# A three-pass half-precision split of the expert layer's first products, with rows turned by the DMA, in a fused attention and mixture-of-experts kernel

## Chip, cores and metric

The kernel runs on 1 core of a Trainium2 chip. The metric is the device time in microseconds (us) of one execution.

## The reference, cut to what matters

Input x has 8 batches of 512 tokens of 128 features (4096 tokens). First attention with 16 heads of 64, causal, with one null key and value, and a layer norm of the sum:

```
x1 = layernorm(x + attention(x))
```

Then a mixture of 32 experts (4 chosen per token out of 4 of 8 groups, at most 640 rows per expert) beside one shared expert, and a second layer norm:

```
w, idx = gate(x1)                     # softmax, grouped top 4, weights normalized
xe = x1 rows by expert                # (32, 640, 128)
h = silu(xe @ w1) * (xe @ w3)         # the first products, 128 to 128
out = (h @ w2) * weight of the row    # added back to the token's row: y
z = silu(x1 @ sw1) * (x1 @ sw3) @ sw2
result = layernorm(x1 + y + z)
```

All is float32.

## The kernel before

All engines follow one list of steps, written by `plan`: each engine runs through `steps` and takes the ones that are its own, in order, so a wait holds up all that stands behind it on that engine. The orders of the attention stage (`ORDER` to `ORDER4`) are written out by hand; the smaller work of a finished batch (`finish`) is put into the slots `place` and `slow`.

- Attention, batch by batch. TensorE, in float16 halves, is busy nearly throughout. ScalarE takes exponentials and copies, VectorE row maxima and low halves, GpSimd the low halves of the probabilities (L2289), SyncE moves keys and queries between partitions (L2458, L2425) and turns the halves of x with one transposing DMA per batch (L2403).
- `finish(b)`: layer norm to X1 (float32), x1 turned on TensorE (L1393), copied to X1T and stored in HBM as columns (L2477, `x1_t`), gate, top 4, places. `payload` on ScalarE (L1690) writes each x1 row four times into PAY (128 float32 values, then the place number and the weight, `ROW` = 130 words), and GpSimd scatters them by 16 indirect DMAs a batch into `xe_rows` (L2322).
- Between the stages SyncE reloads x1's columns (L2483), the weights of the first experts (L2370, then L2491 and L2494) and the rows of the first two experts (L2379). The last batch is finished in two halves of 8 scatters. Five `shared up` / `shared down` steps and the first two experts are worked in between.
- The expert loop, x_ from 2 to 29, in this order on TensorE: `turn(x_+1)` turns the next expert's 640 rows by five float32 transposes into PSUM (L1137), VectorE (`turned`, L1751 and L1752) copies them to XET; `dense_down` (L1488) of the step before; `hidden(x_)` (L1154), four float32 products of 128x320; `dense_up` (L1479), two float32 products of 128x512; `product(x_-1)` (L1167). The dense steps, one in each of x_ = 6 to 24, are the shared expert and two experts computed for all tokens. ScalarE: silu (L1543, L1708) and weighted copies to OUT (L1551). VectorE: products with silu (L1758, L2145) and the dense sums (L2163). GpSimd: five indirect DMAs an expert that scatter OUT's rows to `y_rows` (L2332). SyncE: weights of x_+3 and rows of x_+4; the rows wait until the scatters of expert x_-2 have landed. OUT has 4 buffers and the rows have 6.
- After the last scatter and the last dense sum the token's four rows are loaded, summed (L1523, L1531, L1532) and normalized.

Of the kernel before, what the change touches and what calls it, by code (L numbers as in the profile page):

```python
# [16 lines left out]
N = NB * T  # L17
# [132 lines left out]
def plan(count):  # L150
# [6 lines left out]
        "c_pz", "c_as", "c_dz", "c_nm", "c_sh", "c_na", "c_ps", "c_dl", "c_sc0", "c_lq", "c_k20", "c_k21", "c_k22", "c_ll", "c_xd")}  # L157
# [245 lines left out]
    def finish(b, *half):  # L403
# [59 lines left out]
        if whole or half == (1,):  # L463
            mark("xts", b, by="c_xts", n=16)
# [10 lines left out]
        for h in half:  # L475
            step("payload", b, h)
            mark("payx", b, h, by="c_aj")
            mark("payi", b, h, by="c_pg")
        yield from wait(5)
        for name in ("group max", "group top", "group drop", "masked", "top", "top index"):  # L480
            dv(name)
            yield
        dv("gate sum")
# [42 lines left out]
        if whole:  # L526
            for h in (0, 1):
                step("payload", b, h)
                mark("payx", b, h, by="c_aj")
                mark("payi", b, h, by="c_pg")  # L530
                yield
            ready.append(b)
# [246 lines left out]
    for x_ in range(NA):  # L779
        step("load early rows", x_)  # L780
    gate_free = (st_free[0], st_free[1])
# [43 lines left out]
    step("early turn", 0)  # L825
# [3 lines left out]
    step("early turn", 1)  # L829
# [11 lines left out]
    step("first turn")  # L841
# [11 lines left out]
def program(nc, ctx, x, Wq, Wk, Wv, Wo, null_k, null_v, logit_scale, wg, w1, w2, w3, sw1, sw2, sw3, out):  # L853
# [8 lines left out]
    x1t_d = nc.dram_tensor("x1_t", (C, N), F32, kind="Internal").ap()  # L862
# [105 lines left out]
    def at(*key):  # L968
# [19 lines left out]
    s_turn, s_xet, s_hid, s_sil, s_hs, s_o, s_oc = (  # L988
        sem(n) for n in ("s_turn", "s_xet", "s_hid", "s_sil", "s_hs", "s_o", "s_oc"))
# [52 lines left out]
    ph1, X1TA, HZ, ph2 = flat(K1), flat(K2), flat(Q1), flat(Q2)  # L1042
# [7 lines left out]
    XE = ph2[:, 0:3900].rearrange("p (s k r) -> p s k r", s=6, k=5)  # L1050
    XET = PF[:, 0:2, 0:640]
    SIL = Y[:, :, :, :].rearrange("p s a b -> p s (a b)")
    xe_e = xe.rearrange("(e p k) r -> e p k r", e=E, k=5)
# [28 lines left out]
    BUF = [t[:, h:h + 2048] for t in (X1TA, ph2, HZ, ph1) for h in (0, 2048)]  # L1082
# [39 lines left out]
    def tensor(e):  # L1122
# [1442 lines left out]
```

## Time and profile before

| | us |
|---|---|
| three runs | 977.4, 980.4, 985.9 |
| median | 980.4 |
| span of the profiled execution (first to last instruction) | 977.5 |
| attention, one batch of the middle | 75.7 |
| end of attention to first scatter of expert outputs | 640 to 695 |
| expert stage, scatters of experts 0 to 29 | 695 to 937 |
| load, sum, norm and store | 941 to 977 |

TensorE is busy for 859.0 us of the span, GpSimd 673.5, VectorE 654.3, ScalarE 616.8; the mean granted TensorE clock is 0.943 of full speed. Only the span stands for the profiled execution; what lies outside it is at most the few us by which the runs differ from it.

### The profile page before, as it was taken

What the parts mean: (1) busy time and instruction counts of PE and PEld (TensorE: products, weight loads), DVE (VectorE), ACT (ScalarE), POOL (GpSimd) and SP (SyncE); (2) the same over time, 40 slices, a digit from 0 to 9 for tenths busy, and PEclk for the clock granted to TensorE, in tenths of its full rate; (3) what the DMA queues carried; (4) which work ended last, traced back from release to release, by engine and by line L of the source; (5) the groups of instructions that cost most, each with busy time, mean ns of one, the idle gap of its engine ahead of it and who ended that gap; (6) DMA issues with size and microseconds to landing.
All of it is one profiled execution on the core that took longest, in us unless ns stands there. A gap on an engine that the chain in (4) does not pass through costs nothing. (4 is left out here: it accounts for less than half of the span.)

```text
span 977.5 us, 25690 instructions
## 1 busy us (share of the span) xinstructions
PE 859.0 (88%) x9439; PEld 633.9 (65%) x9439; DVE 654.3 (67%) x2448; ACT 616.8 (63%) x1189; POOL 673.5 (69%) x580
## 2 busy tenths in 40 slices
PE   5789999999999999999999999766688888888654
PEld 2367777777777777777777777654465666666422
DVE  7757788987987987987987986836243434343217
ACT  3668889888888888888898787733132323233305
POOL 7656665699698699699689689346665555556636
PEclk9989999999999999999999999978798989899968
DMA  5787788645444454354354342016333323333147
GB/s 160 182 255 234 231 243 220 177 107 134 97 119 111 101 135 108 89 151 107 73 141 122 72 117 64 21 51 197 119 96 100 96 79 95 95 101 99 39 191 252
DMA packets 104428, 126.62 MB, mean 130 GB/s; under 512 B 22077, under 2 KB 65426, under 8 KB 103408
## 3 DMA queue, kind: packets, MB, share of 16 engines
q1 hardware_dynamic: 95408, 109.25, 40.8%
q0 software_dynamic: 8896, 15.74, 5.2%
q8 instruction: 75, 1.23, 0.5%
q14 instruction: 49, 0.40, 0.1%
HBM read 33.68 MB, written 41.58 MB: 77 GB/s over the span
## 5 line engine op out<-in xcount | busy, mean ns | idle before, releaser
L2289 POOL TENSOR_TENSOR PL<-PF,PH 128x1280 f16<-128x1280 f32 x121 | 317.8, 2626 | 107.2 <-ACT PH L1632 63.7
L1854 DVE CUSTOM_DVE_ANT_0 JUNK<-PS,M 128x256 f16<-128x256 f32 (+3 forms) x512 | 225.2, 485 | 39.5 <-PE PS L1265 35.8
L1626 ACT ACTIVATE PF<-PS 128x512 f32<-128x512 f32 (+1 forms) x384 | 192.8, 520 | 80.3 <-PE PS L1298 75.4
L2332 POOL DMA_INDIRECT y_rows<-BIG,Q x150 | 145.7, 972 | 99.3 <-ACT BIG L1551 57.4
L1632 ACT ACTIVATE PH<-PF 128x1280 f16<-128x1280 f32 x128 | 162.2, 1267 | 0.6
L2322 POOL DMA_INDIRECT xe_rows<-PAY,DEST x128 | 129.3, 1010 | 42.9 <-issue 27.7
L1291 PE MATMUL PS<-Q,K 128*128 128x512 f16 (+3 forms) x512 | 148.6, 300 | 9.2 <-DMA Q<-MROW 4.9
L1315 PE MATMUL PS<-VH,PH 128*128 128x65 f16 x1280 | 141.3, 195 | 13.0 <-DVE Y L1896 8.5
L1317 PE MATMUL PS<-VH,PL 128*128 128x65 f16 x1280 | 141.3, 194 | 1.2 <-issue 1.2
L1315 PEld LDWEIGHTS PS<-VH,PH 128*128 128x128 f16 x1280 | 119.6, 98 | 35.0 <-issue 24.5
L1316 PE MATMUL PS<-VL,PH 128*128 128x64 f16 x1280 | 141.3, 194 | 0.0
L1316 PEld LDWEIGHTS PS<-VL,PH 128*128 128x128 f16 x1280 | 118.8, 99 | 2.7
L1317 PEld LDWEIGHTS PS<-VH,PL 128*128 128x128 f16 x1280 | 119.2, 98 | 0.4 <-issue 0.4
L1296 PE MATMUL PS<-Q,K 65*128 65x128 f16 (+2 forms) x384 | 106.0, 276 | 0.0
L1298 PE MATMUL PS<-Q,K 128*128 128x128 f16 x512 | 102.6, 220 | 0.0
L1294 PE MATMUL PS<-LATER,IDB 128*128 128x64 bf16 x512 | 98.7, 193 | 0.0
L1543 ACT ACTIVATE Y<-PS 128x640 f32<-128x640 f32 x30 | 21.1, 704 | 106.6 <-remote 56.8
L1154 PE MATMUL PS<-PF,K 128*128 128x320 f32 x240 | 80.1, 481 | 9.2 <-DVE Q L2122 4.9
L1154 PEld LDWEIGHTS PS<-PF,K 128*128 128x128 f32 x240 | 49.2, 217 | 29.4 <-issue 16.2
L1291 PEld LDWEIGHTS PS<-Q,K 128*128 128x128 f16 x512 | 50.7, 99 | 24.2 <-ACT PF L1626 8.7
L1265 PE MATMUL PS<-K,Q 64*128 64x256 f16 (+3 forms) x512 | 63.1, 305 | 0.1
L1551 ACT ACTIVATE BIG<-PS,Q 128x128 f32<-128x128 f32 x150 | 42.3, 374 | 30.8 <-PE PS L1167 16.9
(252 smaller groups left out, 2027.5 us busy)
## 6 DMA issues: line engine op xcount, KB each, us to landing
K<-KH SPq DMA_DIRECT2D x128, 128.0 KB, 2.3
Q<-QH SPq DMA_DIRECT2D x128, 128.0 KB, 2.4
xe_rows<-PAY SPq DMA_DIRECT2D x20, 520.0 KB, 4.2
Q<-xe_rows SPq DMA_DIRECT2D x30, 325.0 KB
K<-KL SPq DMA_DIRECT2D x64, 128.0 KB, 2.3
Q<-QL SPq DMA_DIRECT2D x64, 128.0 KB, 2.3
y_rows<-PAY SPq DMA_DIRECT2D x16, 512.0 KB, 4.9
K<-in_L_ffn_w_dram SPq DMA_DIRECT2D x96, 64.0 KB
```

The costliest lines, as they stand in the source:

```text
L1154: i = e.matmul(PS[:, bank + hf, 0:320], EW[:, x_ % 4, m, :], XET[:, x_ % 2, hf * 320:(hf + 1) * 320], start=True, stop=True)
L1291: e.matmul(PS[:, k, o:o + LEN[i]], K1[:, u % 4, ab, pp, block], Q1[:, u % 4, ab, pp, i * 128:512], start=True, stop=False)
L1296: e.matmul(PS[:, k, o + 128:o + LEN[i]], K2[0:65, u % 4, ab, pp, block], Q2[0:65, u % 4, ab, pp, i * 128 + 128:512], start=False, stop=False)
L1315: e.matmul(PS[:, 4, o:o + 65], PH[:, n % PBUF, p], VH[:, vs, i, h, :], start=(i == 0), stop=False)
L1316: e.matmul(PS[:, 4, o:o + 64], PH[:, n % PBUF, p], VL[:, vs, i, h, :], start=False, stop=False)
L1317: r = e.matmul(PS[:, 4, o:o + 65], PL[:, n % PBUF, p], VH[:, vs, i, h, :], start=False, stop=(i == q))
L1626: e.activation(PF[:, n % PBUF, c0:c0 + width], PS[:, k, 0:width], ACT.Exp).then_inc(s["c_exp"], 1)
L1632: e.activation(PH[:, n % PBUF, :], PF[:, n % PBUF, :], ACT.Copy).then_inc(s["c_hc"], 1)
L1854: e.tensor_tensor_reduce(JUNK[:, n_ttr % 2, 0:width], PS[:, base + ab, c0:c0 + width], M0[:, 512 - width:512], 1.0, -3e38, ALU.add, ALU.ma ...
L2289: e.tensor_tensor(PL[:, n % PBUF, :], PF[:, n % PBUF, :], PH[:, n % PBUF, :], ALU.subtract).then_inc(s["c_lp"], 1)
L2322: e.indirect_dma_start(out=xe[:, :] if b < NB - 1 else xe[0:(NE - NA) * CAP, :], out_offset=bass.IndirectOffsetOnAxis(ap=DEST[:, q, k:k + ...
L2332: e.indirect_dma_start(out=y4[:, :], out_offset=bass.IndirectOffsetOnAxis(ap=XE[:, x_ % 6, k, 128:129].bitcast(I32), axis=0), in_=OUT[:, x ...
```

## The change

x1 is no longer kept for the expert stage as float32: `x1 high` (ScalarE) writes its float16 rounding and `x1 low` (VectorE) the float16 rounding of the rest, side by side in the first of the four payload rows. SyncE copies that row to the other three by DMA (`payload`, six DMAs a batch of 128 partitions x 1 KB, waited for by the scatters), and stores x1's rows to HBM (`x1_rows`, 512 bytes a token). In the expert stage the rows arrive turned: `dma_start_transpose` loads an expert's 640 rows x 256 halves into XT, and a second small DMA the place numbers and weights (XI); x1's columns for the shared and dense steps come by transposing DMAs too (512 x 256 each). The float32 transposes on TensorE and their copies by VectorE go. The weights w1, w3 of each expert are split into high and low float16 (`high_weights` on ScalarE, `low_weights` on VectorE, 128x256 each, one expert ahead; the shared and dense ones once). Each first product becomes three float16 products (high x high, high x low of x1, low x high), summed in PSUM. The second products stay float32. Orders of steps are otherwise kept.

```diff
@@ -429,6 +429,11 @@
+        def rows(h):
+            step("payload", b, h)
+            mark("payx", b, h, by=("c_px0", "c_px1")[h], n=48)
@@ -524,11 +534,18 @@
+            step("x1 high", b)
+            mark("x1h", b, by="c_aj")
+            yield
+            dv("x1 low")
+            yield
...
-                step("payload", b, h)
-                mark("payx", b, h, by="c_aj")
+                rows(h)
+                step("place numbers", b, h)
...
+            step("x1 store", b)
+            mark("xts", b, by="c_xts", n=16)
@@ -1047,10 +1067,22 @@
-    XE = ph2[:, 0:3900].rearrange("p (s k r) -> p s k r", s=6, k=5)
+    XT = ph2[:, 0:3840].bitcast(F16).rearrange("p (s w n) -> p s w n", s=6, w=2)
+    XI = ph2[:, 3840:3900].rearrange("p (s k r) -> p s k r", s=6, k=5)
...
-    xe_e = xe.rearrange("(e p k) r -> e p k r", e=E, k=5)
+    xe_t = xe.bitcast(F16).rearrange("(e n) r -> e n r", e=E)
+    XHI = PAY[:, :, 0, 0:64].bitcast(F16)
+    XLO = PAY[:, :, 0, 64:128].bitcast(F16)
+    def split_of(t):
+        return t.bitcast(F16).rearrange("p (w n) -> p w n", w=2)
+    EWS = [split_of(PF[:, j, 0:256]) for j in (0, 1)]
@@ -1126,21 +1158,23 @@
-        def turn(x_):
-            w.wait_ge(l_xe[x_ % 6], 16 * (x_ // 6 + 1))
-            w.wait_ge(s_xet, x_)
-            w.wait_ge(*at("zt", 1))
-            if x_ >= NA:
-                w.wait_ge(*at("z", 3))
-            bank_free(misc_end)
-            for k in range(5):
-                i = e.transpose(five(0, k), XE[:, x_ % 6, k, 0:128], IDF[:, :])
-            i.then_inc(s_turn, 1)
+        def three(out, halves, m, x_of, free):
+            high, low = halves[:, 0, 128 * m:128 * m + 128], halves[:, 1, 128 * m:128 * m + 128]
+            for o, n in free:
+                e.matmul(out(o, n), high, x_of(0, o, n), start=True, stop=False)
+                e.matmul(out(o, n), high, x_of(1, o, n), start=False, stop=False)
+            for o, n in free:
+                i = e.matmul(out(o, n), low, x_of(0, o, n), start=False, stop=True)
+            return i
...
-            w.wait_ge(l_w[x_ % 4], 48 * (x_ // 4 + 1))
-            w.wait_ge(s_xet, x_ + 1)
+            w.wait_ge(l_xe[x_ % 6], 32 * (x_ // 6 + 1))
+            w.wait_ge(s_wsh, x_ + 1)
+            w.wait_ge(s_wsl, x_ + 1)
...
+            if x_ == 0:
+                w.wait_ge(*at("zt", 1))
@@ -1150,15 +1184,15 @@
-                for hf in range(2):
-                    i = e.matmul(PS[:, bank + hf, 0:320], EW[:, x_ % 4, m, :], XET[:, x_ % 2, hf * 320:(hf + 1) * 320],
-                                 start=True, stop=True)
-                i.then_inc(s_hid, 1)
+                three(lambda o, n: PS[:, bank + o // 320, 0:n], EWS[x_ % 2], m, lambda k, o, n: XT[:, x_ % 6, k, o:o + n],
+                      ((0, 320), (320, 320))).then_inc(s_hid, 1)
...
+                bank_free(misc_end)
+                w.wait_ge(l_w[x_ % 4], 48 * (x_ // 4 + 1))
@@ -1440,14 +1473,13 @@
-                e.matmul(PS[:, one, :], SW[:, 0, :], X1TA[:, t], start=True, stop=True)
-                e.matmul(PS[:, two, :], SW[:, 1, :], X1TA[:, t], start=True, stop=True).then_inc(s["c_ph"], 1)
+                for m, bank in ((0, one), (1, two)):
+                    i = three(lambda o, n: PS[:, bank, 0:n], SWS, m, lambda k, o, n: X1TA[:, b, k, :], ((0, 512),))
+                i.then_inc(s["c_ph"], 1)
...
-                if b >= 2:
-                    w.wait_ge(s_xet, 2)
@@ -1544,12 +1571,17 @@
-            w.wait_ge(l_xe[y_ % 6], 16 * (y_ // 6 + 1))
+            w.wait_ge(l_xe[y_ % 6], 32 * (y_ // 6 + 1))
...
-                             scale=XE[:, y_ % 6, k, 129:130]).then_inc(s_oc, 1)
+                             scale=XI[:, y_ % 6, k, 1:2]).then_inc(s_oc, 1)
+        def high_weights(x_):
+            w.wait_ge(l_w[x_ % 4], 48 * (x_ // 4 + 1))
+            w.wait_ge(s_hid, 2 * (x_ - 1))
+            e.activation(EWS[x_ % 2][:, 0, :], EW[:, x_ % 4, 0:2, :].rearrange("p m n -> p (m n)"), ACT.Copy).then_inc(s_wsh, 1)
@@ -1680,16 +1711,21 @@
-            elif name == "payload":
-                b, half = a
-                w.wait_ge(*at("scat", b - 1, half))
+            elif name == "x1 high":
+                b, *half = a
+                q0, q1 = span(*half)
+                for h in half or (0, 1):
+                    w.wait_ge(*at("scat", b - 1, h))
...
-                for key in parts_of("normalize", b, half):
-                    w.wait_ge(*at(*key))
-                for q in (2 * half, 2 * half + 1):
-                    i = e.activation(PAY[:, q, :, 0:128], X1[:, 4 * b + q, :].unsqueeze(1).broadcast_to((128, 4, 128)),
-                                     ACT.Copy)
-                i.then_inc(s["c_aj"], 1)
+                w.wait_ge(*at("xts", b - 1))
+                w.wait_ge(*at("normalize", b, *half))
+                e.activation(XHI[:, q0:q1, :], X1[:, 4 * b + q0:4 * b + q1, :], ACT.Copy).then_inc(s["c_aj"], 1)
+            elif name == "shared split":
+                w.wait_ge(l_sw, 48)
+                w.wait_ge(*at("ng", LAST))
+                e.activation(SWS[:, 0, :], SW[:, 0:2, :].rearrange("p m n -> p (m n)"), ACT.Copy).then_inc(s_dwh, 1)
+            elif name == "early split":
+                high_weights(*a)
@@ -1745,11 +1790,11 @@
-        def turned(x_):
-            w.wait_ge(s_turn, x_ + 1)
+        def low_weights(x_):
+            w.wait_ge(s_wsh, x_ + 1)
...
-            e.tensor_copy(XET[:, x_ % 2, 0:384], PS[:, 0, 0:384])
-            e.tensor_copy(XET[:, x_ % 2, 384:640], PS[:, 1, 0:256]).then_inc(s_xet, 1)
+            e.tensor_tensor(EWS[x_ % 2][:, 1, :], EW[:, x_ % 4, 0:2, :].rearrange("p m n -> p (m n)"), EWS[x_ % 2][:, 0, :],
+                            ALU.subtract).then_inc(s_wsl, 1)
@@ -2109,12 +2153,21 @@
-            elif name == "early turn":
-                turned(*a)
+            elif name == "x1 low":
+                b, *half = a
+                q0, q1 = span(*half)
+                w.wait_ge(*at("x1h", b, *half))
+                e.tensor_tensor(XLO[:, q0:q1, :], X1[:, 4 * b + q0:4 * b + q1, :], XHI[:, q0:q1, :],
+                                ALU.subtract).then_inc(s["c_dv"], 1)
...
@@ -2164,18 +2216,22 @@
+        def low_dense(d):
+            src = DW[:, d, 0:2, :] if d < ND else AW[:, d - ND, 0:2, :]
+            w.wait_ge(s_dwh, d + 2)
+            e.tensor_tensor(DWS[d][:, 1, :], src.rearrange("p m n -> p (m n)"), DWS[d][:, 0, :],
+                            ALU.subtract).then_inc(s_dwl, 1)
...
-            if x_ == NA:
-                times(x_)
-            if x_ < NE - 1:
-                turned(x_ + 1)
+            if x_ + 1 < NE:
+                low_weights(x_ + 1)
...
-            if x_ > NA:
-                times(x_)
+            times(x_)
...
+                low_dense(WEIGHTS[k])
@@ -2374,9 +2430,10 @@
-            w.wait_ge(s_turn, x_ - 5)
+            w.wait_ge(s_hid, 2 * (x_ - 5))
...
-            e.dma_start(XE[:, x_ % 6, :, :], xe_e[expert(x_)]).then_inc(l_xe[x_ % 6], 16)
+            e.dma_start_transpose(XT[:, x_ % 6, :, :], xe_t[expert(x_)][:, 0:256]).then_inc(l_xe[x_ % 6], 16)
+            e.dma_start(XI[:, x_ % 6, :, :], xe_i[expert(x_)][:, :, 128:130]).then_inc(l_xe[x_ % 6], 16)
@@ -2470,17 +2527,27 @@
-            elif name == "x1 copy" and a != [NB - 1, 0]:
-                b = a[0]
-                for key in parts_of("x1t", b):
+            elif name == "payload":
+                b, half = a
+                q = slice(*span(half))
+                key = (b,) if b < NB - 1 else (b, half)
+                w.wait_ge(*at("x1h", *key))
+                w.wait_ge(*at("x1 low", *key))
+                w.wait_ge(*at("scat", b - 1, half))
+                for k in range(1, 4):
+                    i = e.dma_start(PAY[:, q, k, 0:128], PAY[:, q, 0, 0:128])
+                    i.then_inc(s[("c_px0", "c_px1")[half]], 16)
+            elif name == "x1 store":
+                b, = a
+                for key in parts_of("x1 low", b) + parts_of("x1h", b):
...
-                e.dma_start(x1t_d[:, b * 512:(b + 1) * 512], X1T[:, :]).then_inc(s["c_xts"], 16)
+                e.dma_start(x1_b[b], PAY[:, :, 0, 0:128].bitcast(F16)).then_inc(s["c_xts"], 16)
...
-                e.dma_start(X1TA[:, b * 512:(b + 1) * 512], x1t_d[:, b * 512:(b + 1) * 512]).then_inc(l_xa[b], 16)
+                e.dma_start_transpose(X1TA[:, b, :, :], x1_d[b * 512:(b + 1) * 512, :]).then_inc(l_xa[b], 16)
```

`dense_up` calls `three` in the same way; the splits of the shared and dense weights and the place numbers' step on GpSimd are left out here.

## Rows read from the trace of the kernel before

**Rows 1.** Busy time by stage: stretch, its length, busy us of each engine, TensorE's clock, DMA share, GB/s
```profile
225.70:301.40 75.70, 74.59 (x1043) 56.85 (x1042) 64.43 (x264) 64.05 (x117) 62.25 (x49) 1.00 0.44 111
...
745.00:897.00 152.00, 132.74 (x625) 96.39 (x625) 61.51 (x137) 46.57 (x124) 86.17 (x90) 0.90 0.32 93
...
941.00:977.50 36.50, 23.99 (x54) 11.21 (x54) 18.97 (x92) 13.16 (x32) 18.67 (x18) 0.78 0.78 288
```

**Rows 2.** Timeline of GpSimd, expert stage: start, us, instruction, idle before it
```profile
712.13 0.97 POOL L2332 DMA_INDIRECT y_rows<-BIG,Q  x1 [2.80 <-ACT BIG L1551]
...
743.08 0.97 POOL L2332 DMA_INDIRECT y_rows<-BIG,Q  x1 [3.46 <-ACT BIG L1551]
...
760.12 0.97 POOL L2332 DMA_INDIRECT y_rows<-BIG,Q  x1 [0.68 <-issue]
...
769.40 0.97 POOL L2332 DMA_INDIRECT y_rows<-BIG,Q  x1 [3.20 <-ACT BIG L1551]
...
896.66 0.97 POOL L2332 DMA_INDIRECT y_rows<-BIG,Q  x1 [2.91 <-ACT BIG L1551]
...
935.82 0.97 POOL L2332 DMA_INDIRECT y_rows<-BIG,Q  x1 [0.30 <-issue]
```

**Rows 3.** Timeline, TensorE in one pass of the expert loop, full clock
```profile
752.89 0.71 PE L1137 MATMUL PS<-IDF,Q 128*128 128x128 f32 x5
...
753.66 1.16 PE L1488 MATMUL PS<-SW,Q 128*128 128x128 f32 x8
...
754.65 2.32 PE L1154 MATMUL PS<-PF,K 128*128 128x320 f32 x8
...
756.81 1.88 PE L1479 MATMUL PS<-K 128*128 128x512 f32 x4
...
758.53 1.28 PE L1167 MATMUL PS<-K 128*128 128x128 f32 x10
```

**Rows 4.** The same timeline one pass later, VectorE and ScalarE behind TensorE
```profile
763.37 0.56 DVE L1751 COPY PF<-PS 128x384 f32<-128x384 f32 x1 [3.95 <-remote]
...
767.68 0.70 ACT L1543 ACTIVATE Y<-PS 128x640 f32<-128x640 f32 x1 [6.80 <-remote]
```

**Rows 5.** Timeline, TensorE in the pass after that, half clock
```profile
771.07 1.91 PE L1488 MATMUL PS<-K,Q 128*128 128x128 f32 x8
```

**Rows 6.** Timeline of TensorE, attention: two neighbouring float16 products
```profile
232.84 0.39 PE L1234 MATMUL PS<-XHL,WKH 128*128 128x512 f16 x1
...
233.06 0.38 PE L1234 MATMUL PS<-XHL,WKL 128*128 128x512 f16 x1
```

**Rows 7.** SyncE's timeline at a transposing DMA (256 KB)
```profile
270.41 1.27 SPq L2403 DMA_TRANSPOSE XHL<-BIG  x1
```

**Rows 8.** Busy time in the us in which its packets run, columns as in rows 1
```profile
272.00:273.00 1.00, 1.00 (x32) 0.93 (x29) 1.00 (x4) 0.88 (x3) 1.00 (x1) 1.00 1.02 201
```

**Rows 9.** Timeline of SyncE between the stages
```profile
656.68 3.20 SPq L2483 DMA_DIRECT2D K<-x_t  x7
659.92 6.12 SPq L2370 DMA_DIRECT2D K<-in_L_ffn_w_dram  x12
...
671.86 0.85 SPq L2379 DMA_DIRECT2D Q<-xe_rows  x2
...
693.10 3.18 SPq L2379 DMA_DIRECT2D Q<-xe_rows  x2
```

**Rows 10.** Timeline of GpSimd: the last of the 16 scatters of the last batch
```profile
690.79 0.97 POOL L2322 DMA_INDIRECT xe_rows<-PAY,DEST  x1 [0.30 <-issue]
```

**Rows 11.** The page, DMA issues: KB each, median us from issue to landing
```profile
K<-KH SPq DMA_DIRECT2D x128, 128.0 KB, 2.3
```

**Rows 12.** The payload copies' line: ns min/median/max, first and last start
```profile
L1690 ACT ACTIVATE PAY<-X x32: 610/614/661, 186.1 to 669.3; 128x512 f32<-128x512 f32 x32
```

**Rows 13.** The waits in the attention stage: us in total, times, longest
```profile
PE PS L1291 <- DMA Q<-MROW: 2.3, 3, 1.0
```

**Rows 14.** The chain that ended last: start, us, what
```profile
939.90 1.14 DVE X L2163 x4
...
941.18 9.74 PE PS L1523 x16
```

More of the change, by code:

```diff
@@ L474, in finish @@
         mark("ex", b, *half, by="c_aj")
-        for h in half:
-            step("payload", b, h)
-            mark("payx", b, h, by="c_aj")
-            mark("payi", b, h, by="c_pg")
+        if not whole:
+            step("x1 high", b, *half)
+            mark("x1h", b, *half, by="c_aj")
+            step("place numbers", b, *half)
+            mark("payi", b, *half, by="c_pg")
         yield from wait(5)
@@ L482, in finish @@
             yield
+        if not whole:
+            dv("x1 low")
+            rows(half[0])
+            if half == (1,):
+                step("x1 store", b)
+                mark("xts", b, by="c_xts", n=16)
         dv("gate sum")
@@ L780, in plan @@
         step("load early rows", x_)
+    step("shared split")
     gate_free = (st_free[0], st_free[1])
@@ L824, in plan @@
         next(parts[b])
-    step("early turn", 0)
+    step("early split", 0)
+    step("early split", 1)
     next(parts[2])
@@ L828, in plan @@
     step("early hidden", 0)
-    step("early turn", 1)
+    step("early split", 2)
     next(parts[3])
@@ L840, in plan @@
     next(parts[4])
-    step("first turn")
     next(parts[4])
@@ L1424, in tensor @@
                 i.then_inc(s["c_pm"], 1)
-            elif name == "first turn":
-                turn(NA)
             elif name == "shared up":
                 b, = a
-                t = slice(b * 512, (b + 1) * 512)
                 w.wait_ge(l_xa[b], 16)
                 w.wait_ge(l_sw, 48)
+                w.wait_ge(s_dwh, 1)
+                w.wait_ge(s_dwl, 1)
                 if b < 2:
@@ L1458, in tensor @@
                 i.then_inc(s["c_pz"], 1)
-            elif name == "early turn":
-                turn(*a)
             elif name == "early hidden":
@@ L1478, in dense_up @@
             for m, bank in ((0, one), (1, two)):
-                e.matmul(PS[:, bank, :], weights(d, m), X1TA[:, t], start=True, stop=True).then_inc(s_dup, 1)
+                three(lambda o, n: PS[:, bank, 0:n], SWS if d == SHARED else DWS[d], m, lambda k, o, n: X1TA[:, b, k, :],
+                      ((0, 512),)).then_inc(s_dup, 1)
         def dense_down(i, rows):
             d, b = DENSE[i]
+            w.wait_ge(l_dw, 48 * (ND + NA))
             w.wait_ge(s_dh, i + 1)
@@ L1714, in scalar @@
                 copies(x_)
+            for k in WEIGHTS_AT.get(x_, ()):
+                high_dense(WEIGHTS[k])
             if x_ in DENSE_AT:
@@ L1763, in shared_add @@
             w.wait_ge(*at("down", b))
-            w.wait_ge(*at("payx", b, 1))
-            for key in parts_of("xT1", b):
+            for key in parts_of("x1h", b) + parts_of("x1 low", b) + parts_of("xT1", b):
                 w.wait_ge(*at(*key))
@@ L2151, in dense_add @@
                 w.wait_ge(*at("z", b))
-            w.wait_ge(*at("payx", b, 1))
-            for key in parts_of("xT1", b):
+            for key in parts_of("x1h", b) + parts_of("x1 low", b) + parts_of("xT1", b):
                 w.wait_ge(*at(*key))
@@ L2306, in gpsimd @@
                 e.tensor_tensor(RS[:, q], VE[:, q], MHALF[:, q], ALU.pow).then_inc(s["c_pg"], 1)
-            elif name == "payload":
+            elif name == "place numbers":
                 b, half = a
@@ L2498, in sync @@
             if x_ > NA:
[L2499 removed]
+                w.wait_ge(l_xe[x_ - 1], 32)
             load_rows(x_)
```

63 lines of the change are left out of this document (35 added, 28 removed).

## The prediction

> **What bounds the kernel now.** I read the busy times by stage first, then GpSimd's timeline in the expert stage, then one pass of the loop on TensorE. In attention TensorE is busy for 74.6 of 75.7 us a batch [rows 1]: that stage is TensorE's, and nothing on ScalarE, VectorE or SyncE shortens it. In the expert stage the scatters are the clock to read. They follow each other at 0.97 + 0.30 = 1.275 us while OUT is full, so five cost 6.38 us; the first scatter of expert 2 is at 712.1, of expert 6 at 743.1, of expert 24 at 896.7, the last one at 935.8 [rows 2]. That is 7.74 us an expert from 2 to 6, 8.53 from 6 to 24, and 39.2 us from there to the last scatter, 29 steps on. The gaps end with ScalarE's copies [rows 2], and these wait for TensorE: it, not GpSimd, bounds the dense stretch (132.7 of 152 us busy) [rows 1]. A pass at full clock has 6.75 us of it: turn 0.55 + 0.33 to the next group, dense_down 0.89, hidden 2.15, dense_up 1.72, product 1.11 (from start to start of the groups; a group's own time has a tail that overlaps the next) [rows 3].
>
> But three passes take 3 x 8.53 = 25.6 us, not 20.3. In one of three VectorE and ScalarE get TensorE's results late: the copy of the turned rows waits 3.95 us and silu 6.80 us for something the trace doesn't name, though TensorE's records lie where they should [rows 4]; the pass after it runs at half clock (dense_down's group 1.91 instead of 1.16 us) [rows 3, 5]. The scatters show a pass of 9.3 us (760.12 to 769.40) [rows 2]; with one of 6.75 the third has 9.6, so about 2.5 us and 2.8 us are lost in each three passes. It begins when GpSimd goes on from one expert's scatters to the next without a pause (0.68 us at 760.12) [rows 2]. I don't know its cause; it is what the prediction depends on.
>
> **The change, part by part.**
> TensorE, expert loop. The turn goes (0.88 us with its gap) [rows 3]. Hidden: 4 float32 products become 12 float16 ones. Two neighbouring float16 products of 512 columns start 0.216 us apart [rows 6], so one of 320 columns is worth 0.135 and hidden 1.63 us instead of 2.15; dense_up 6 x 0.216 = 1.29 instead of 1.72. dense_down of the step before now stands right behind product and waits for three copies by ScalarE, which the turn covered: I take the same 0.88 us of waiting. A pass: 0.88 + 0.89 + 1.63 + 1.29 + 1.11 = 5.8 us, under the scatters' 6.38. With neither late results nor half clock the pace would be GpSimd's 6.38.
>
> VectorE and ScalarE, loop. VectorE loses 0.97 us of copies and gets a subtraction of 128x256; ScalarE gets a copy of 128x256. Bounds of each: 0.37 (0.56 scaled down by width) and 0.61 [rows 4, 12]. Both engines are busy for 62 and 47 of 152 us [rows 1], so I cost them at nothing; they are done one expert ahead, behind no wait that isn't a pass old. The wait for hidden's first group goes from VectorE's copy to a DMA: one round trip fewer between TensorE and VectorE (three a pass become two), so a late pass loses less.
>
> Pace. I take 5.8 us for a pass that isn't disturbed, and still one late and one half-clock pass, each with two thirds of the old loss and a loss that GpSimd's backlog of 0.6 us a pass doesn't hide: about 7.2 us an expert. Lower bound 6.38, upper bound the present 8.53. From 6 to 24: 18 x 7.2 = 129.6 instead of 153.6: **-24.0 us** (-38.8 to 0).
>
> SyncE between the stages, a loss. Its queue is in order. Seven loads of x1's columns take 3.20 us of issue; turned they are transposing DMAs of 1024 packets like x's, 1.27 us each: 8.9 [rows 7, 9]. The weights stay: 659.9 to 671.9 [rows 9]. The first two rows loads take 0.85; turned they are 1.25 times x's, 1.6, with 0.4 for the numbers: 4.0. So SyncE is free at 656.7 + 8.9 + 12.0 + 4.0 = 681.6 instead of 672.7. Behind it stands the new `payload` of the last batch's first half: three moves, 0.5 us each, landing 2.3 us after the last issue [rows 11]: 685. GpSimd's scatters wait for it; the 16th starts 15 x 1.275 later, at 704.1 instead of 690.8 [rows 10], 13.3 us late. The rows of expert 2 are asked for 2.3 us after the last scatter's start now (693.1) [rows 9, 10], then at 706.4, and are there by 711. But GpSimd has experts 0 and 1 to scatter from 705.4 to 718.2, ready since, so expert 2's first scatter is at about 718.4 instead of 712.1: **+6.3 us** (0 if SyncE issues faster, +13 if nothing closes up). From 2 to 6, no dense steps, GpSimd has backlog and runs at 6.38: 25.5 instead of 31.0: **-5.5 us** (-5.5 to 0).
>
> End. The last dense sum ends at 941.0, 4.2 us after the last scatter [rows 2, 14]. TensorE's tail is now shorter and starts earlier, so the scatters' landing (936.8 + 1.4) would be last: **-2.5 us** (-2.8 to 0). The final stage's 36.5 us [rows 1] stay.
>
> Attention. ScalarE gives up 4 copies of 0.61 us a batch [rows 12] for one; VectorE gets one of 512 columns; neither sets the pace [rows 1]. SyncE gets 6 moves a batch at some 0.6 us, behind waits for `x1 high` and `x1 low`; key and query moves and the row of maxima stand behind them. TensorE has waited for that row 3 times, 2.3 us in all [rows 13]. I take **+1 us** (0 to +35, seven batches at 5). Indirect scatters now wait for a DMA, but GpSimd has 13 us of slack a batch [rows 1].
>
> Transposing DMAs as such. x's 256 KB are issued in 1.27 us, and in the us from 1.6 us after the issue on the queues move at 201 GB/s [rows 7, 8]: some 3.4 us in all, 4.3 for an expert's 320 KB. They are asked for some four passes ahead, so they are hidden; the source there was SBUF, though, and no row has one from HBM.
> The Trainium skill (VectorE: DVE Perf Modes, The three transpose paths) gives 1309 ns for a 128x128 transpose by DMA; x's move has eight such tiles and the trace has it far faster than eight times that, while the same skill (Advanced Engine Details and Errata, X-Bar Transpose) calls these DMAs as fast as regular ones. By the first an expert's ten tiles would be an estimated 13 us and the kernel over 100 us slower; by the second nothing changes in the sum.
>
> Sum: -24.0 + 6.3 - 5.5 - 2.5 + 1.0 = -24.7 on the span of 977.5: 952.8. The median of the runs is 2.9 us above that span: **955.7 us**.
>
> **Rivals.**
> *A, the pace doesn't move.* The late results and the half clock set 8.5 us, not TensorE's work. For it: a lighter pass leaves GpSimd even less pause, the state in which the lateness begins [rows 2, 4]. Against: a third of the round trips go. Then +6.3 - 5.5 + 1: 982 us.
> *B, GpSimd's pace throughout*, no late passes: a further -14.8: 941 us.
> *C, row loads become the bound (the slower side).* Five DMAs an expert instead of four on SyncE, one transposing from HBM, one of 8-byte pieces. If a load takes over twice the 4.3 us of the SBUF case, the pace is over 8.5, the point from which it decides; at 10 us it is 27 x (10 - 7.2) = +76: 1030 us. For it: no row shows such a source. Against: rows 7 and 8. The skill's 1309 ns a tile is this case.
> *D, attention slips* because SyncE's in-order queue delays the row of maxima [rows 13]: 5 us in each of seven batches: 990 us.
> *E, TensorE stays at half clock* since it is busy for less: hidden 3.3, dense_up 2.6, dense_down 1.6, product 2.2, waits 0.9: 10.6 us a pass (its slow groups are those of [rows 5]): +61 on 955.7: 1017 us.
>
> **Chances.** Forecast 0.60, B 0.13, A 0.12, C 0.07, D 0.05, E 0.03. Faster by over 1% (below 970.6; about 1% is what a measurement tells from no change): forecast and B, 0.73; within 1%: A, and a forecast that falls short, 0.13; slower 0.14. The range takes B's time and A's with their doubts: 937 to 985; the forecast alone 943 to 970.
>
> **What would show it.** Scatters of expert 2 at 716 to 721 and of expert 24 at 868 to 875; SyncE's first row load near 678, the last batch's first scatter near 685; pairs of expert scatters without a pause more often than now; VectorE without waits of 4 us for a turn; attention at 75.7 us a batch. The prediction is wrong if the scatters stay 8.5 us apart with TensorE idle (A), if hidden waits for DMA landings (C), if a batch takes over 77 us (D), or if the granted clock between 745 and 890 is under 0.7 (E).

## The result, and the profile after

The changed kernel takes 1026.8 us (median of four runs, 1025.5 to 1030.0), the kernel before 979.8 beside it: a ratio of 1.0475, 95% interval 1.0437 to 1.0513. It is slower by 47 us (46.2 between the two profiled spans) where I forecast 24.7 us less.

The profiled execution spans 1023.7 us instead of 977.5. Four landmarks cut it up, the same that the prediction used. In both kernels SyncE's first load of x1 between the stages waits for the end of attention; before it was at 656.68 [rows 9].

SyncE's timeline of the changed kernel:

```profile
692.90 1.30 SPq L2550 DMA_TRANSPOSE K<-x_rows  x1
...
717.62 0.58 SPq L2436 DMA_DIRECT2D Q<-xe_rows  x1
718.64 4.00 SPq L2538 DMA_DIRECT2D PAY<-PAY  x6
```

GpSimd's timeline of the changed kernel, the lines that answer to [rows 10] and [rows 2]: the last scatter of x1 rows, then the first scatters of experts 2, 6 and 24, and the last one:

```profile
744.39 0.97 POOL L2378 DMA_INDIRECT xe_rows<-PAY,DEST  x1 [0.30 <-issue]
...
758.43 0.97 POOL L2388 DMA_INDIRECT y_rows<-BIG,Q  x1 [0.30 <-ACT BIG L1578]
...
795.09 0.97 POOL L2388 DMA_INDIRECT y_rows<-BIG,Q  x1 [4.14 <-ACT BIG L1578]
...
945.79 0.97 POOL L2388 DMA_INDIRECT y_rows<-BIG,Q  x1 [1.46 <-ACT BIG L1578]
...
986.71 0.97 POOL L2388 DMA_INDIRECT y_rows<-BIG,Q  x1 [0.30 <-issue]
```

| stretch | before | after | difference | forecast |
|---|---|---|---|---|
| start to first x1 load (attention) | 656.7 | 692.9 | +36.2 | +1.0 |
| from there to expert 2's first scatter | 55.4 | 65.5 | +10.1 | +6.3 |
| experts 2 to 6 | 31.0 | 36.7 | +5.7 | -5.5 |
| experts 6 to 24 | 153.6 | 150.7 | -2.9 | -24.0 |
| from there to the end | 80.8 | 77.9 | -2.9 | -2.5 |
| sum | 977.5 | 1023.7 | +46.2 | -24.7 |

So there are two questions: who takes 36 us in attention, and what happened to the 24 us of the expert loop.

**Attention.** The page of the changed kernel, its costliest groups (busy, mean ns, idle just before and what ended it):

```profile
L2378 POOL DMA_INDIRECT xe_rows<-PAY,DEST x128 | 129.0, 1008 | 103.9 <-DMA PAY<-PAY 61.5
...
L1299 PE MATMUL PS<-K,Q 64*128 64x256 f16 (+3 forms) x512 | 63.8, 308 | 21.7 <-DVE MXV L1898 18.0
```

and the same two groups on the page of the kernel before:

```profile
L2322 POOL DMA_INDIRECT xe_rows<-PAY,DEST x128 | 129.3, 1010 | 42.9 <-issue 27.7
...
L1265 PE MATMUL PS<-K,Q 64*128 64x256 f16 (+3 forms) x512 | 63.1, 305 | 0.1
```

GpSimd sits idle for 61.5 us ahead of scatters of x1's rows until the new copies of the payload row have landed, and TensorE waits 18.0 us for VectorE's row maxima (MXV); before, there was no such wait. The timeline of one batch, lines of four engines put in order of time, shows both:

```profile
351.22 2.61 POOL L2345 TENSOR_TENSOR PL<-PF,PH 128x1280 f16<-128x1280 f32 x1 [0.91 <-issue]
352.11 2.27 DVE L2160 TENSOR_TENSOR PAY<-X,PAY 128x512 f16<-128x512 f32 x1 [0.46 <-ACT PAY L1722]
355.05 0.39 PE L1299 MATMUL PS<-K,Q 64*128 64x256 f16 x4 [2.32 <-DVE MXV L1898]
355.75 1.99 SPq L2538 DMA_DIRECT2D PAY<-PAY  x3
360.49 1.03 POOL L2378 DMA_INDIRECT xe_rows<-PAY,DEST  x1 [6.66 <-issue]
365.56 0.19 PE L1349 MATMUL PS<-VH,PH 128*128 128x65 f16 x1 [1.81 <-issue]
```

VectorE's subtraction for x1's low half (L2160) takes 2.27 us. It began while GpSimd worked on the low halves of p (L2345) and ended 0.55 us after GpSimd had ended at 353.83. So it is in each of the first six batches (2.27 us each, always beside such an operation of GpSimd). In the seventh GpSimd stands idle at that time, and the same subtraction is short:

```profile
669.55 0.68 DVE L2160 TENSOR_TENSOR PAY<-X,PAY 128x512 f16<-128x512 f32 x1
```

The Trainium skill (SBUF — State Buffer, SBUF: two separate sides) has a rule for this that I had not used: a VectorE operation with two SBUF inputs and a GpSimd operation that reads SBUF lock each other out for a whole instruction. By that rule the subtraction has to stand behind GpSimd's; the trace agrees (2.27 us beside 0.68). Then the DMA copies are issued at 355.75, GpSimd has stood still since 353.83, and the scatter goes at 360.49. The first scatter of a batch waits like this for 6.3 to 7.5 us in six batches, and for 17.8 and 16.0 in the last two. Behind it in GpSimd's queue stand the next low halves of p (362.81 to 365.46), for which the products of L1349 wait until 365.56.

**Expert loop.** The windows of the changed kernel, columns as in [rows 1], at the same clock times and at the end:

```profile
745.00:897.00 152.00, 102.39 (x574) 74.22 (x574) 47.42 (x104) 50.17 (x136) 89.53 (x91) 0.81 0.49 102
990.00:1023.70 33.70, 22.62 (x52) 9.46 (x51) 18.82 (x91) 13.16 (x32) 18.67 (x18) 0.91 0.84 309
```

The first window is not the same work as before: here experts 0 to 6 fill its first 50 us. Experts 6 to 24, which had 132.7 busy us of TensorE [rows 1], now run from 795 to 945, with 107.9 at a granted clock of 0.88 (the row stands with e4 below). So TensorE's work did fall, and still an expert takes 8.37 us. The late results of [rows 4] are there: TensorE's products of hidden end at 812.76, and ScalarE's silu starts 5.8 us later, held by something that the trace does not name (it writes `remote`). TensorE's line, then ScalarE's:

```profile
812.33 0.43 PE L1168 MATMUL PS<-Q,PF 128*128 128x320 f16 x2
...
818.58 0.70 ACT L1570 ACTIVATE Y<-PS 128x640 f32<-128x640 f32 x1 [6.46 <-remote]
```

TensorE waits for ScalarE's copies ahead of dense_down, and goes in and out of half clock (1.96 us for a group that takes 1.13 at full clock):

```profile
872.90 1.96 PE L1520 MATMUL PS<-K,Q 128*128 128x128 f32 x8 [3.15 <-ACT BIG L1578]
...
881.05 1.13 PE L1520 MATMUL PS<-K,Q 128*128 128x128 f32 x8 [1.32 <-ACT BIG L1578]
...
889.24 1.30 PE L1520 MATMUL PS<-K,Q 128*128 128x128 f32 x8 [3.03 <-ACT BIG L1578]
```

### The profile page after: what moved, and what is told of

Read it like the earlier page. It is cut to its first block, busy times and chain, and to the rows that moved or that the text cites. A ratio compares the mean times of both kernels' runs of the same rounds, so it can differ in the third digit from the quotient of the medians.

```text
span 1023.7 us, 25899 instructions
## 1 busy us (share of the span) xinstructions
PE 832.3 (81%) x9461; PEld 611.4 (60%) x9461; DVE 653.1 (64%) x2432; ACT 618.3 (60%) x1201; POOL 675.4 (66%) x580
## 4 chain that ended last, share of the span: by engine, by line
PE 52%; ACT 9%; issue 9%; SPq 8%; another core or an unknown queue 7%; DMA 6%; DVE 5%; POOL 3%; ACTq 0%; POOLq 0%; DVEq 0%
PE PS L1268 6%; PE PS L1325 5%; PE PS L1299 4%; PE PS L1349 3%; PE PS L1378 3%; PE PS L1332 3%; PE PS L1330 3%; PE PS L1351 3%; PE PS L1350 3%; PE PS L1282 2%; SPq L2515 2%; PE PS L1379 2%; PE PS L1201 2%; PE PS L1520 2%
## 5 line engine op out<-in xcount | busy, mean ns | idle before, releaser
L2345 POOL TENSOR_TENSOR PL<-PF,PH 128x1280 f16<-128x1280 f32 x121 | 318.0, 2628 | 103.3 <-ACT PH L1664 67.0
L2388 POOL DMA_INDIRECT y_rows<-BIG,Q x150 | 148.4, 989 | 93.9 <-ACT BIG L1578 54.2
L2378 POOL DMA_INDIRECT xe_rows<-PAY,DEST x128 | 129.0, 1008 | 103.9 <-DMA PAY<-PAY 61.5
L1349 PE MATMUL PS<-VH,PH 128*128 128x65 f16 x1280 | 141.8, 196 | 19.8 <-issue 8.5
L1349 PEld LDWEIGHTS PS<-VH,PH 128*128 128x128 f16 x1280 | 119.9, 98 | 44.9 <-issue 25.5
L1803 DVE TENSOR_TENSOR K<-PS,Y 128x640 f32<-128x640 f32 x30 | 24.7, 824 | 73.9 <-PE PS L1168 27.0
L1201 PE MATMUL PS<-K 128*128 128x128 f32 x300 | 45.7, 307 | 27.9 <-issue 9.3
L1325 PEld LDWEIGHTS PS<-Q,K 128*128 128x128 f16 x512 | 50.5, 99 | 25.7 <-ACT PF L1658 10.3
```

The costliest lines, as they stand in the source:

```text
L1325: e.matmul(PS[:, k, o:o + LEN[i]], K1[:, u % 4, ab, pp, block], Q1[:, u % 4, ab, pp, i * 128:512], start=True, stop=False)
L1349: e.matmul(PS[:, 4, o:o + 65], PH[:, n % PBUF, p], VH[:, vs, i, h, :], start=(i == 0), stop=False)
L2345: e.tensor_tensor(PL[:, n % PBUF, :], PF[:, n % PBUF, :], PH[:, n % PBUF, :], ALU.subtract).then_inc(s["c_lp"], 1)
L2378: e.indirect_dma_start(out=xe[:, :] if b < NB - 1 else xe[0:(NE - NA) * CAP, :], out_offset=bass.IndirectOffsetOnAxis(ap=DEST[:, q, k:k + ...
L2388: e.indirect_dma_start(out=y4[:, :], out_offset=bass.IndirectOffsetOnAxis(ap=XI[:, x_ % 6, k, 0:1].bitcast(I32), axis=0), in_=OUT[:, x_ % ...
```

## The experiments

Eighteen runs, in five groups of three or four, each group on one chip beside the kernel before. For attention the theories are S (GpSimd waits for the payload DMAs), V (VectorE's subtraction stands behind GpSimd) and Q (SyncE's queue delays the other moves); for the expert loop L (late results set the pace), C (the clock does) and rival C of the prediction (row loads). A batch is the time from the first scatter of x1 rows of one batch to that of the next, as a mean over five; it was 75.8 us before and 81.8 after. Several kernels leave out part of the work, as their expectations say; they are timed only to learn what that part costs.

### Attention

**e1**: the payload rows written by ScalarE.

```diff
-                for k in range(1, 4):
-                    i = e.dma_start(PAY[:, q, k, 0:128], PAY[:, q, 0, 0:128])
+                for q in (2 * half, 2 * half + 1):
+                    i = e.activation(PAY[:, q, 1:4, 0:128].bitcast(F16), ...broadcast_to((128, 3, 256)), ACT.Copy)
```

> The changed kernel with one part undone: rows 1 to 3 of the payload are written by ScalarE again (four float16 copies of 128x768 a batch) instead of six DMAs on SyncE. A batch of attention takes 81.9 us in the changed kernel and 75.7 in the one before. Theory S (GpSimd's in-order queue waits for the payload DMAs and the low halves of p behind it come late): a batch falls to about 77 to 78, the kernel to about 990. Theory V (VectorE's subtraction of 128x512 takes 2.27 us because it stands behind GpSimd's, and TensorE waits 2.3 us for the row maxima behind it): most of the 6.2 us stays, a batch 80 or more, the kernel about 1010 to 1020. Theory Q (SyncE's queue is what delays keys, queries and the row of maxima): a batch at 75.7, the kernel about 980.

Measured: a batch 79.4 us; 990.8 us beside 970.5, ratio 1.022 (1.013 to 1.032). That is between what theories S and V foretold. Of theory S it is not all: GpSimd still waits 3 us a batch, now for ScalarE's copies.

```profile
271.57 1.03 POOL L2386 DMA_INDIRECT xe_rows<-PAY,DEST  x1 [3.03 <-ACT PAY L1728]
```

**e2**: DMAs as they are, the scatters later in the list.

```diff
             mark("xts", b, by="c_xts", n=16)
+            for _ in range(4):
+                yield
             ready.append(b)
```

> The changed kernel with the scatters of a batch put into GpSimd's list four slots of the batch's smaller work later, all DMAs kept. Theory S: GpSimd no longer waits for the payload DMAs, a batch at 77 to 79 us instead of 81.9, the kernel about 1000. Theory Q: the DMAs are still on SyncE's queue, so a batch stays at 80 to 82 us and the kernel at 1020 or more.

Measured: a batch 78.3 us, 1010.0 us, ratio 1.042 (1.031 to 1.053). The scatter finds its rows ready (no idle time before it):

```profile
279.95 1.03 POOL L2380 DMA_INDIRECT xe_rows<-PAY,DEST  x1
```

The six DMAs stayed on SyncE's queue and 3.5 us of the 6.0 went: the queue as such (theory Q, the prediction's rival D) is not the cause, GpSimd's wait is.

**e3** and **e3b**: the subtraction left out in the first seven batches, with the DMAs and with ScalarE's copies.

> The changed kernel, but for the first seven batches VectorE's subtraction that makes x1's low half is left out (ScalarE writes the rounded x1 in its place, so the low half is not the rest), DMAs and waits kept. Theory V: TensorE's wait of 2.3 us a batch for the row maxima goes, a batch at about 79.6 us instead of 81.9. Theory S alone: no more than 0.5 us a batch.

> The payload rows written by ScalarE and, for the first seven batches, the subtraction left out as well. If S and V are all there is, a batch is back at 75.7 to 76.3 us. If it stays above 77, something else in the change costs time in attention (ScalarE's 3.4 us of copies a batch are the candidate).

Measured: 82.8 us a batch in e3, 77.6 in e3b (1030.8 and 991.8 us, one run each). With the DMAs in place nothing is won by leaving the subtraction out. TensorE's waits for the row maxima did fall, from 3.0 us a batch to 0.7, but its waits without a named releaser, such as the one at 365.56 above, rose from 1.5 to 4.9: GpSimd's wait takes up what was won. With the DMAs gone the subtraction is worth 1.8 us.

**e7**: e2, and the subtraction moved to GpSimd's list.

```diff
-            dv("x1 low")
+            dv("x1 low", by="c_pg")
...
+            elif name == "x1 low" and len(a) == 1:
+                e.tensor_tensor(XLO[:, :, :], X1[:, 4 * b:4 * b + 4, :], XHI[:, :, :], ALU.subtract)
```

> The changed kernel with the scatters four slots later and the subtraction that makes x1's low half moved from VectorE to GpSimd for the first seven batches, all DMAs kept. Theories S and V together: a batch at 76 to 77 us instead of 81.9 (78.3 with the later scatters alone), the kernel at about 995 to 1000. If VectorE's 2.27 us subtraction did not matter, a batch stays at 78.3 or more.

Measured: a batch 75.6 us, 987.5 us beside 975.2, ratio 1.016 (1.006 to 1.025). Attention is whole again; TensorE is busy for 74.6 of 76 us as in [rows 1], with all DMAs in place:

```profile
272.90:348.90 76.00, 74.56 (x1047) 57.02 (x1046) 64.55 (x265) 62.96 (x113) 62.98 (x50) 1.00 0.49 124
```

### The expert loop

**e4**: TensorE kept busy where it stood idle.

```diff
+            if rows < 5 * (NE - 1):
+                w.wait_ge(s_sil, (rows - 3) // 5 + 2)
+            for _ in range(8 if rows < 5 * (NE - 1) else 0):
+                e.matmul(PS[:, 2, :], SWS[:, 0, 0:128], X1TA[:, 0, 0, :], start=True, stop=True)
             w.wait_ge(s_oc, rows)
```

> The changed kernel; ahead of the wait of each dense_down TensorE makes eight more float16 products of 128x512 into a bank of PSUM that is free (1.7 us at full clock, results not used), where it now stands idle 1.3 to 3 us. Theory C (the idle time brings the half clock, and the half clock costs the 1.5 us a pass): the granted clock from expert 6 to 24 rises from 0.86 to over 0.95 and an expert takes 7.4 us or less instead of 8.37. Theory L (the late results set the pace, the half clock only follows them): no more than 0.3 us an expert is won. If the extra products land on the path, an expert takes up to 1.7 us more.

Measured: 1028.1 us beside 975.2, ratio 1.058 (1.048 to 1.067). The granted clock rose from 0.88 to 0.97 over the same 150 us (the changed kernel, then e4):

```profile
795.00:945.00 150.00, 107.92 (x640) 80.35 (x641) 53.85 (x120) 52.78 (x142) 89.19 (x90) 0.88 0.45 97
```

```profile
795.00:945.00 150.00, 127.98 (x799) 85.85 (x799) 53.31 (x120) 53.90 (x147) 89.66 (x91) 0.97 0.46 97
```

and experts 6 to 24 took 148.7 us instead of 150.7. That total alone does not tell, since the filler can cost what the clock gives back: in eight of the 18 passes the copy that dense_down waits for had ended 0.7 to 3.7 us before it. But in five neighbouring passes it ended less than 0.1 us before each dense_down, so that the filler delayed nothing, and they have full clock throughout:

```profile
879.03:920.32 41.29, 34.57 (x221) 23.14 (x221) 15.19 (x35) 15.03 (x41) 24.57 (x25) 1.00 0.47 99
```

That is 8.26 us a pass, with ScalarE's copies still held by something unnamed. The half clock is not what sets the pace, and theory C falls.

**e5**: GpSimd's scatters of the expert rows left out; SyncE has one plain DMA an expert instead.

```diff
+        def store_out(x_):
+            w.wait_ge(s_oc, 5 * x_ + 5)
+            e.dma_start(y5[x_], OUT[:, x_ % 4, :, :]).then_inc(s_ys[x_ % 4], 16)
```

> The changed kernel with GpSimd's 150 scatters of the expert rows left out: SyncE stores each expert's weighted rows with one plain DMA of 320 KB into a tensor that nobody reads, so the sums at the end lack the experts. Theory L (TensorE's results come late because GpSimd issues indirect DMAs back to back): waits for something unnamed on VectorE and ScalarE vanish, an expert takes 6.3 to 6.8 us instead of 8.37. Theory C: the idle time of TensorE is there without GpSimd, so half clock and 8 us an expert stay.

Measured: 937.4 us (one run). An expert takes 5.87 us, evenly, at full clock, with no waits for something unnamed, which is less than the 6.3 to 6.8 that I expected. Two neighbouring silu steps on ScalarE, and 72 us of the stage:

```profile
820.99 0.70 ACT L1571 ACTIVATE Y<-PS 128x640 f32<-128x640 f32 x1 [1.31 <-PE PS L1169]
826.86 0.70 ACT L1571 ACTIVATE Y<-PS 128x640 f32<-128x640 f32 x1 [1.30 <-PE PS L1169]
```

```profile
790.00:862.00 72.00, 63.58 (x447) 48.40 (x446) 37.99 (x88) 36.44 (x98) 0.00 (x0) 1.00 0.66 148
```

**e10**: the same cut in the kernel before.

> The kernel before with GpSimd's 150 scatters of expert rows left out, SyncE storing each expert's rows with one plain DMA, so the sums at the end lack the experts. The changed kernel with the same left out has an expert at 5.9 us. The prediction's 6.75 us for a pass of the kernel before says 6.7 to 7.0 us here; then TensorE's saving of 0.9 us is real and is hidden by what the scatters do. If an expert is at 5.9 to 6.1 us here too, the change saves nothing on TensorE.

Measured: 6.75 us an expert.

```profile
732.80 0.70 ACT L1544 ACTIVATE Y<-PS 128x640 f32<-128x640 f32 x1 [1.81 <-PE PS L1155]
739.55 0.70 ACT L1544 ACTIVATE Y<-PS 128x640 f32<-128x640 f32 x1 [1.81 <-PE PS L1155]
```

The two passes of the prediction, 6.75 and 5.8 us, are 6.75 and 5.87. TensorE's saving is real; with the scatters there it is not had on the chip of the result.

**e6**: row loads of the same bytes, not transposing.

```diff
-            e.dma_start_transpose(XT[:, x_ % 6, :, :], xe_t[expert(x_)][:, 0:256])
+            e.dma_start(XT[:, x_ % 6, ...], xe_p[expert(x_)][:, :, 0:256])
```

> The changed kernel; the 30 row loads are plain DMAs of the same bytes (five pieces of 512 bytes a partition) instead of transposing ones, so the experts work on rows that are not turned. Rival C of the prediction (row loads become the bound): experts 2 to 6 take 31 us or less instead of 36.7, since hidden waits there for xe_rows, and 6 to 24 fall by 10 us or more from 150.7. If the transposing DMAs are hidden: both stretches as they are, within 3 us.

Measured: 1017.7 us (one run); experts 2 to 6 in 30.0 us (36.7 with transposing loads), 6 to 24 in 145.0 (150.7); but from the first scatter to expert 2's it took 4.3 us more. From the first to expert 24's scatter that is 192.1 instead of 200.1 us. This does not show that the transposing loads cost 8 us, for runs that keep them come as low: e1 has 31.1, 146.2 and 192.6 us for the same three stretches, e3 has 30.8, 146.0 and 193.1. A transposing load from HBM is not slow by itself. The view of DMAs of the changed kernel has x1's, 256 KB each, at 4.0 us from issue to landing; it has no landing time for the experts' row loads of 320 KB, but that of e14 (below), on a chip of the same kind, has:

```profile
K<-x_rows SPq DMA_TRANSPOSE x8, 4.0
```

```profile
Q<-xe_rows SPq DMA_TRANSPOSE x30, 4.6
```

4.6 us there and 3.8 in e5 are near the 4.3 that the prediction took from x's move, and far below the 8.6 at which rival C begins.

**e9** and **e14**: GpSimd issues its 150 DMAs, but plain ones; one kernel, on two chips.

```diff
-                e.indirect_dma_start(out=y4[:, :], out_offset=..., in_=OUT[:, x_ % 4, k, :], ...)
+                e.dma_start(y5[x_, :, k, :], OUT[:, x_ % 4, k, :])
```

> The changed kernel; GpSimd still issues 150 DMAs of 64 KB in the expert stage, but plain ones to fixed rows of a tensor that nobody reads, so the sums at the end lack the experts. Theory G (any DMA that GpSimd issues back to back makes TensorE's results late): waits for something unnamed stay, an expert at 7.5 to 8.4 us. Theory I (it is the indirect ones, by their work on GpSimd of 0.97 us each or by their packets): an expert at 5.9 to 6.1 us as without GpSimd, no such waits.

Measured: 932.0 us, 5.9 us an expert. In the same group e8 (below), with indirect scatters, has no unnamed waits in its dense stretch either, and the kernel before took 906.3 us (904.4 to 908.7 in 11 runs) where it had taken 964 to 986 up to then. So e9 told nothing, and chips had become a question of their own. The next group took both kernels along, on a chip where the kernel before is at 979.1 (e11 is the kernel before with a trace, e12 the changed kernel):

> The kernel before once more, for its trace on the chip of this call: in the last call it took 906 us where it had taken 970 to 980, and no trace of it was taken there. Theory H (chips differ in the late results and the half clock): where it takes about 906, an expert from 6 to 24 takes 6.8 us (TensorE's pass) and VectorE and ScalarE have no waits for something unnamed; where it takes 970 or more, 8.5 us with such waits, and attention is the same within 1 us a batch in both.

> The changed kernel on the same chip. Its loss in attention and between the stages (47 us) does not depend on the chip. On a chip with a time before of about 906 an expert takes 6.4 us (GpSimd's pace) instead of 6.8, so the kernel is at about 945 to 950, 4 to 5% slower; on one with 970 or more it is at 1015 to 1027, 4.5 to 5% slower.

> The kernel of e9 (GpSimd issues 150 plain DMAs in place of the indirect ones) on the same chip. It had 5.9 us an expert on a chip on which e8 had no late results either, so it told nothing. On a chip where the kernel before takes 970 or more: theory G (any DMA that GpSimd issues) 7.5 to 8.4 us an expert with waits for something unnamed; theory I (the indirect ones alone) 5.9 to 6.1 us. Where the kernel before takes about 906, it tells nothing again.

Measured: e11 976.2 us, 152.7 us for experts 6 to 24; e12 1031.9 us beside 979.1, ratio 1.058 (1.045 to 1.070), a little above what I expected, 148.0 us for experts 6 to 24; e14 950.9 us (one run), 5.9 us an expert, full clock, no unnamed wait in the dense stretch:

```profile
790.00:862.00 72.00, 63.61 (x444) 48.13 (x443) 37.02 (x83) 36.73 (x97) 32.72 (x62) 1.00 0.74 148
```

On one chip, then, 8.2 us an expert with indirect scatters and 5.9 with plain ones from the same engine: theory I. Plain ones are also cheaper for GpSimd (0.54 us instead of 0.97), so this does not tell apart what the indirect DMA does from how long it does it.

**e15, e16, e17** were to tell that apart.

> The changed kernel; of an expert's five scatters three stay indirect, the last two are plain DMAs by GpSimd into a tensor that nobody reads, so the sums at the end lack those rows. On a chip where the kernel before takes 970 or more: theory R (each indirect DMA costs a share of lateness, some 1.65 us of pace) says 5.9 to 6.3 us an expert; theory P (lateness needs a pause too short between two experts' scatters, and GpSimd now pauses 2 us) says 5.9 us and no waits for something unnamed at all.

> The same with four of five scatters indirect (the fifth row tile is missing from the sums). Theory R: about 6.7 us an expert, with late results. Theory P: GpSimd needs 4 x 1.28 + 0.84 = 5.96 us for its five, so it still goes on without a pause beside a TensorE pass of 5.9 us, and lateness stays: 7 us or more.

> The changed kernel; the 150 indirect DMAs stay, but their row numbers are consecutive (row = 128 x number of the scatter + partition) and go to a tensor that nobody reads, so the sums at the end lack the experts. If the scattered addresses in HBM bring the late results, an expert takes 6.4 us, GpSimd's pace. If it is the indirect DMA as an instruction of GpSimd, an expert stays at 8.2 to 8.5 us with waits for something unnamed.

Measured: 5.9, 5.9 and 6.4 us an expert (937.5, 944.3, 960.1 us, one run each), on a chip where the kernel before took 906.0. There late results are rare whatever the scatters do, so the three leave their question open. What e17 does show is GpSimd's pace: 90 steps of 1.286 us from expert 6 to 24, 115.7 us, with no pause.

```profile
769.81 0.97 POOL L2393 DMA_INDIRECT y_plain<-BIG,NUMB  x1 [0.30 <-issue]
...
885.55 0.97 POOL L2393 DMA_INDIRECT y_plain<-BIG,NUMB  x1 [0.30 <-issue]
```

### The mended kernel

**e8** is e7 with the last batch's payload by ScalarE, out of SyncE's queue; **e13** is the same kernel on the chip of e11 and e12.

> The changed kernel with the later scatters, the low half's subtraction on GpSimd for seven batches, and the payload rows of the last batch written by ScalarE, so that they no longer stand behind SyncE's loads between the stages. In the run before it (e7) the first x1 load is at 654.5, the first expert scatter 52.7 us after it; where ScalarE wrote the payload (e1) that was 43.9. If SyncE's in-order queue is what holds the last batch back, the first expert scatter comes at 698 to 700 instead of 707.2 and the kernel takes 12 us less than e7's 987.5, some 975, within 1% of the kernel before. If something else holds it, it stays within 3 us of e7.

> The kernel of e8 (scatters later, low half on GpSimd, the last batch's payload by ScalarE) on the same chip. In the last call it was 0.7% slower than the kernel before, at 906 us. On a chip with 970 or more before, e7's 987.5 less the 8 to 12 us that the last batch's payload is worth: 975 to 980, ratio 0.995 to 1.01.

Measured: e8 912.0 us beside 906.3, ratio 1.0067 (1.0049 to 1.0085); e13 982.3 beside 979.1, ratio 1.011 (0.999 to 1.023). The first expert scatter comes 45.5 us after the first x1 load in e13 (52.7 in e7, 38.6 before): 7 of the 14 us between the stages come back. It beats the kernel before on neither chip. In the traces of e13 and of the kernel before, attention ends 6.8 us earlier in e13 and the stretch behind it is as much longer, so the first expert scatter comes at the same time (695.4 and 695.3); experts 6 to 24 take 149.5 us instead of 153.6. The profiled run of e13 was the fastest of its four (976.9, median 982.3), so where the median loses that again no trace shows. I found no version that beats the kernel before.

## Why the prediction was wrong, point by point

- **What bounds the kernel.** Attention is TensorE's, that held; but I took from its 74.6 busy us of 75.7 that nothing on the other engines could lengthen it. Being the bound means the opposite: TensorE has no slack, so an operand that comes late enough lengthens the batch.
- **Attention, +1 us: the step that failed first.** I wrote "Indirect scatters now wait for a DMA, but GpSimd has 13 us of slack a batch". The slack is an average; the queue is in order, the wait falls in one piece of 6.3 to 7.5 us, and the low halves of p stand behind it. Measured +36.2, just above the term's own range (0 to +35). Of the 6 us a batch, 3.5 are this wait (e2) and 2.8 the subtraction (e7 beside e2), which I had costed at nothing since VectorE is not the bound.
- **Rival D** had the place (attention slips) and a size (5 us a batch), but the wrong mechanism: SyncE's queue with the DMAs in it costs at most what is left in e7, nothing (75.6 us).
- **TensorE's pass, 5.8 us, and 6.75 before**: right (e5: 5.87, e10: 6.75).
- **Pace, 8.53 to 7.2 us: the second step that failed.** Measured 8.37. "One late and one half-clock pass, each with two thirds of the old loss" had no row behind it. The loss hangs on GpSimd's indirect scatters (e14 and e5 beside e12), and it took up the whole saving; how it does so stays open. Rival A is what happened on the chip of the result (-2.9 us instead of -24.0); its argument, that a lighter pass leaves GpSimd less pause, was not tested. Rival B, GpSimd's 6.38 us, is what happened on the other chips (e8: 115.2 us from 6 to 24).
- **Experts 2 to 6, -5.5**: measured +5.7. I had GpSimd's backlog hold a pace of 6.38 there, as if late results came with the dense steps only. They come before them too: in the changed kernel expert 7's silu, still ahead of expert 6's first scatter, waits 7.74 us for something unnamed.

```profile
793.37 0.70 ACT L1570 ACTIVATE Y<-PS 128x640 f32<-128x640 f32 x1 [7.74 <-remote]
```

  With the same row loads, e14 takes 24.7 us for this stretch, and e8, where no wait is unnamed, 25.7 beside my 25.5. With indirect scatters on the slower kind of chip it took 30.8 to 38.0, a spread that no run explains. **Rival C**, row loads as the bound, is not what happened: they land in 3.8 to 4.6 us (e5, e14).
- **SyncE between the stages, +6.3**: measured +10.1. From the first x1 load to the end of the row loads I had 24.9 us, it was 25.3; the payload DMAs stand behind them as forecast (718.64). The last scatter of x1 rows comes 51.5 us after the first x1 load instead of 34.1, 17.4 us later where I had 13.3: the first of the 16 starts 30.2 us after that load (forecast 28.3), and GpSimd stands idle for 2.2 us before the second, as it did in the kernel before, which my 15 steps of 1.275 left out.
- **End, -2.5**: measured -2.9, in part by luck. From the last scatter to the loads of the final stage it takes 2.2 us instead of 5.4, near the forecast; but the final stage, which I had left as it was, takes 1.5 less, and from expert 24's first scatter to the last one it takes 1.8 more.
- **Rival E**, half clock throughout: not so, the granted clock is 0.88 from expert 6 to 24, and e4's passes at full clock are no faster.

## What to carry to other kernels

A DMA or an operation that an in-order engine waits for is priced by what stands behind it in that queue, not by the engine's slack; put its consumer several slots later and it cost nothing here (e2, e7: no wait ahead of the scatters). Before a VectorE operation with two SBUF inputs is costed at nothing, look at what GpSimd does at that time. And where a loop has a loss of unknown cause, forecast both that it stays whole and that it goes, not a share of it: here it went with GpSimd's indirect scatters, and the saving on TensorE did not get past it.

## What was not expected of the hardware

- With GpSimd's 150 indirect DMAs in the loop, on the slower kind of chip, ScalarE and VectorE get some of TensorE's results late: silu starts up to 6.9 us after the record of its products ends (expert 7 of the changed kernel; 5.0 us in each third pass before). With as many plain DMAs from GpSimd (e14), or none (e5), it never does in the dense stretch: it starts 0.04 us after them. Why is open, and whether their number, their length or their packets matter (e15 to e17 ran where it does not show).
- It depends on the chip: the kernel before took 964 to 987 us on the chip of the result and those of three groups, and 904 to 909 on the two of the others. The traces from those two (e8, e17) show 6.4 us an expert, with instructions of the same length (0.97 us a scatter, spaced 1.28). A batch of attention differs by about 1 us. Neither kernel itself has a trace from the faster kind, and the changed kernel was timed only on the slower one.
- The loop gained nothing from full clock: 8.26 us a pass at 1.00 (e4) beside 8.37 at a mean of 0.88.
